# All mixture units of the first two batches run inside the adjacency loop, a slot every second step, and nine groups are combined there

## The reference, cut to what matters

```python
# x: 8192 x 128, adj: 8192 x 8192, all float32
msg = layernorm(x) @ W + B
weights = where(adj < 1.0, exp(-(1/adj - 1)**2 / (2 * 0.5**2)), 0.0)
x = x + weights @ msg
# mixture of experts on layernorm(x): 16 experts, 2 per row, hidden 256
logits = n @ gate_w + gate_b;  top2 = top_k(logits, 2);  share = softmax(top2)
moe = sum_k share_k * (relu(n @ w1[e_k] + b1[e_k]) @ w2[e_k] + b2[e_k])
x = x + layernorm(n + moe) * gamma + beta
```

## Time and profile before

| what | value |
| --- | --- |
| median of 3 runs | 1727.93 us (1727.41 to 1729.02) |
| the profiled execution, its own time | 1725.96 us |
| its span in the trace | 1724.2 us |
| PE busy (matmul) | 1605.5 us, 93% |
| ACT busy | 1563.5 us, 91% |
| DVE busy | 1494.9 us, 87% |
| POOL busy | 538.3 us, 31% |
| mean share of the 16 DMA engines that is busy, q1 | 66.5% |

### The profile page before, as it was taken

One profiled execution on the slowest core, in us unless ns is written; L12 is line 12 of the kernel. 1 busy time (PEld: TensorE's weight loads), 2 busy tenths in 40 slices (PEclk: granted clock), 3 DMA queues, 4 the chain that ended last, 5 costly groups with the idle time before them and its releaser, 6 DMA issues.

```text
span 1724.2 us, 24880 instructions
## 1 busy us (share of the span) xinstructions
PE 1605.5 (93%) x8327; PEld 1069.9 (62%) x8327; DVE 1494.9 (87%) x2312; ACT 1563.5 (91%) x1530; POOL 538.3 (31%) x354
## 2 busy tenths in 40 slices
PE   4999999999999999999999999999998998988870
PEld 3666666666666666656666666666665665757760
DVE  7999989898989898999787878878898898877676
ACT  5899999999999999999999999999997998966662
POOL 1001040404040404090303012040464655465773
PEclk9999999999999999999999999999999999999985
DMA  9558976766666766676777777777776886735662
GB/s 322 150 159 261 259 215 204 207 201 209 201 208 202 208 201 208 200 219 199 216 222 222 216 217 208 220 216 222 226 216 189 239 234 200 228 101 148 183 180 82
DMA packets 246236, 354.26 MB, mean 205 GB/s; under 512 B 20896, under 2 KB 103584, under 8 KB 245984
## 3 DMA queue, kind: packets, MB, share of 16 engines
q1 hardware_dynamic: 237792, 335.62, 66.5%
q0 software_dynamic: 8320, 17.06, 3.2%
HBM read 318.99 MB, written 35.73 MB: 206 GB/s over the span
## 4 chain that ended last, share of the span: by engine, by line
PE 73%; DVE 14%; POOL 4%; issue 4%; ACT 2%; DMA 2%; SPq 1%; DVEq 0%; ACTq 0%; POOLq 0%
PE acc L1394 42%; PE tp L1464 21%; DVE chunk L864 4%; POOL early_back L633 4%; DVE chunk L870 3%; PE tp L1440 2%; PE tp L1431 2%; DVE stats L876 1%; PE tp L1491 1%; DVE chunk L1278 1%; PE acc L1508 1%; ACT chunk L824 1%; PE tp L1508 1%; PE misc L1370 1%; DVE msg L939 1%
## 5 line engine op out<-in xcount | busy, mean ns | idle before, releaser
L1394 PE MATMUL acc<-wT,msg 128*128 128x512 f32 x2048 | 974.3, 598 | 1.8 <-DVE yT L970 1.8
L720 ACT ACTIVATE wT<-tp 128x1024 f32<-128x1024 f32 x512 | 636.4, 1326 | 35.8 <-PE tp L1464 35.7
L870 DVE SCALAR_TENSOR_TENSOR chunk<-chunk 128x2048 f32<-128x2048 f32 x256 | 584.2, 2282 | 31.2 <-ACT chunk L713 30.8
L1464 PEld LDWEIGHTS tp<-ident,chunk 128*128 128x128 f32 x4096 | 478.6, 142 | 204.9 <-issue 199.0
L864 DVE SCALAR_TENSOR_TENSOR chunk<-chunk 128x2048 f32<-128x2048 f32 x256 | 583.7, 2281 | 2.0 <-DMA chunk<-in_adj_dram 2.0
L713 ACT ACTIVATE chunk<-chunk 128x2048 f32<-128x2048 f32 x256 | 567.7, 2217 | 0.1
L1464 PE MATMUL tp<-ident,chunk 128*128 128x128 f32 x4096 | 536.7, 274 | 9.5 <-DVE pair_out L1170 8.7
L1394 PEld LDWEIGHTS acc<-wT,msg 128*128 128x128 f32 x2048 | 351.4, 192 | 255.3 <-issue 249.9
L708 ACT ACTIVATE chunk<-chunk 128x4096 f32<-128x4096 f32 x118 | 466.3, 3951 | 2.3 <-DVE chunk L864 2.3
L673 POOL DMA_INDIRECT rows_in<-y,row_now x128 | 254.4, 1988 | 37.3 <-issue 37.3
L607 POOL TENSOR_TENSOR pool_carrier<-pool_carrier 1x1 f32<-1x1 f32 x32 | 29.8, 931 | 720.7 <-DVE row_now L1055 705.0
(11 more groups left out here) (143 smaller groups left out, 940.7 us busy)
## 6 DMA issues: line engine op xcount, KB each, us to landing
chunk<-in_adj_dram SPq DMA_DIRECT2D x256, 1024.0 KB, 5.7
pair_w<-first_layers SPq DMA_DIRECT2D x104, 129.0 KB, 5.1
pair_in<-rows_in SPq DMA_DIRECT2D x104, 64.0 KB
rows_out<-pair_out SPq DMA_DIRECT2D x52, 128.0 KB, 5.8
chunk<-rows_in SPq DMA_DIRECT2D x85, 64.0 KB
rows_out<-chunk SPq DMA_DIRECT2D x41, 128.0 KB
y_kept<-y SPq DMA_DIRECT2D x16, 256.0 KB, 6.1
rows_in<-zeros SPq DMA_DIRECT2D x64, 64.0 KB
```

The costliest lines, as they stand in the source:

```text
L720: act.activation(wT[:, s % WSLOTS, :], tp[place(s) % TSLOTS][:, :], ACT.Exp, scale=-2.0).then_inc(weighted, 1)
L870: dve.scalar_tensor_tensor(out=slot(c), in0=slot(c), scalar=2.0, in1=slot(c), op0=ALU.subtract, op1=ALU.mult).then_inc(squared, 1)
L1394: ins = pe.matmul(acc[:, :], msg[:, n, :], wT[:, (g * PPG + m) % WSLOTS, k * ROWS:(k + 1) * ROWS], start=(n == 0), stop=(n == 2 * PPG - 1))
L1464: ins = pe.transpose(tp[place(s) % TSLOTS][:, t * ROWS + b * P:t * ROWS + (b + 1) * P], chunk[:, c % RING, b, j:j + P], ident[:, :])
```

## The change

All 128 units of the first two batches (72 and 56, the second padded by one) run in slots, and the slots lie two steps apart: from step 272 to 346 and from 432 to 490. 62 units stay behind the loop. Pair rows are loaded as soon as the buffer of three pairs back is free. Nine groups are combined in the loop, at steps 369 to 509, from three half buffers of four parts each (`ones` and `before`, used at the start only, now lie in one of them); POOL waits for one half at a time. The early guess moves from POOL's power to a logarithm and an exponential on ACT. Behind the loop the positions 0 to 15 hold the last group's gate alone; unit v's output is at position 16 + v, and the seven late groups start at 20, 31, 52, 66, 77, 88 and 99. Rows for the units are loaded from position 7 on.

```diff
-    UNITS[0] += UNITS[0] % 2
+    UNITS = [n + n % 2 if b < 2 else n for b, n in enumerate(UNITS)]
...
-    SLOT_EVERY = 4
-    PAIR_FIRST = [0, UNITS[0] // 2]
-    SECOND_PAIRS = 16
-    NP = PAIR_FIRST[1] + SECOND_PAIRS
+    IN_LOOP = 2
+    SLOT_EVERY = 2
+    PAIR_FIRST = [UNIT0[b] // 2 for b in range(IN_LOOP)]
+    NP = UNIT0[IN_LOOP] // 2
...
-    AT_STEP = [(FIRST[b + 1] + 1) * PPG + 21 for b in range(2)]
+    AT_STEP = [(FIRST[b + 1] + 1) * PPG + 16 for b in range(IN_LOOP)]
+    SLOT_STEP = [AT_STEP[b] + SLOT_EVERY * i for b in range(IN_LOOP) for i in range(UNITS[b] // 2 + 2)]
...
+    ROWS_STEP = [SLOT_STEP[n] - 7 if p < 3 or p - 3 < PAIR_FIRST[pair_batch(p)] else SLOT_STEP[n - 3] + 1
+                 for p, n in enumerate(TURN_SLOT)]
+    WEIGHTS_STEP = [SLOT_STEP[n] - 1 for n in TURN_SLOT]
...
-    EARLY_AT = (436, 461, 471, 493, 503)
-    EARLY_GATE = (12, 13, 13, 14, 14)
+    EARLY_AT = (369, 378, 400, 409, 431, 440, 463, 503, 509)
+    EARLY_GATE = (10, 10, 11, 11, 12, 12, 13, 14, 14)
...
-    EARLY_SLOTS = 8
+    EARLY_HALVES = 3
...
-        early_back = sb("early_back", [P, KB, D])
+        early_back = sb("early_back", [P, EARLY_HALVES, TB, D])
+        ones, before = early_back[:, 0, 0, :], early_back[:, 0, 1, :]
...
+        UNIT_AT = 16
+        ROWS_AT = 7
...
+        starts = dict(zip(LATE, (20, 31, 52, 66, 77, 88, 99)))
...
             def gather_early(h):
-                last_carried()
-                if h == 0:
-                    results_there(0)
-                    pool.wait_ge(idx_ready, 1)
-                else:
-                    pool.wait_ge(early_free, h)
-                carry()
-                gather(h, 0, early_back, early_rows)
...
+                b = max(b for b in range(len(BATCHES)) if FIRST[b] <= h)
+                for k in range(K):
+                    q = K * h + k
+                    last_carried()
+                    if h == FIRST[b] and k == 0:
+                        results_there(b)
+                        pool.wait_ge(idx_ready, b + 1)
+                    if q >= EARLY_HALVES:
+                        pool.wait_ge(early_free, q - EARLY_HALVES + 1)
+                    carry()
+                    for t in range(TB):
+                        gather(h, b, k * TB + t, early_back[:, q % EARLY_HALVES, t, :], early_rows[q % EARLY_HALVES])
...
                     if EARLY_GATE[h] == g:
                         gather_early(h)
-                        guess_early(h)
                 if g == GROUPS - 1:
-                    for late in range(EARLY, FIRST[1]):
-                        gather_late(late)
+                    gather_late(EARLY)
+                    gather_late(EARLY + 1)
...
+            def guess_early(h):
+
+                act.wait_ge(early_moments, h + 1)
+                act.activation(early_lnv[:, :], early_mv[:, :, 1], ACT.Ln, bias=eps[:, 0:1]).then_inc(early_lnv_ready, 1)
+                act.wait_ge(early_lnv_ready, h + 1)
+                act.activation(early_rs[:, :], early_lnv[:, :], ACT.Exp, scale=-0.5).then_inc(early_guessed, 1)
...
+                    for h in range(EARLY):
+                        if g * PPG + m == EARLY_AT[h] + 5:
+                            guess_early(h)
...
-            turn_tile(0)
-            turn_tile(1)
             products(GROUPS - 1, PPG - 2)
-            turn_tile(2)
-            turn_tile(3)
-            hidden(0)
             products(GROUPS - 1, PPG - 1)
-            hidden(1)
-            for i in range(max(NT, PPG)):
+            for i in range(UNIT_AT + NT):
```

More of the change, by code:

```diff
@@ L83, in gnn_moe_kernel @@
     ALL_TURNED = place(STEPS - 1) + 1
-    def pair_batch(p):
-        return 1 if p >= PAIR_FIRST[1] else 0
     NT = NU - NE
@@ L131, in gnn_moe_kernel @@
         ident = sb("ident", [P, P])
-        ones = sb("ones", [P, P])
-        before = sb("before", [P, P])
         eps = sb("eps", [P, 1])
@@ L307, in gnn_moe_kernel @@
         pair_stored = [sem(f"pair_stored{i}") for i in range(2)]
-        early_rows = sem("early_rows")
+        early_rows = [sem(f"early_rows{i}") for i in range(EARLY_HALVES)]
         early_free = sem("early_free")
@@ L551, in _ @@
             for i in range(LAST + 2):
-                if 1 <= i <= NT:
-                    store_rows(i - 1)
-                if i + RIN < NT:
-                    load_rows(i + RIN)
+                if 0 <= i - UNIT_AT - 1 < NT:
+                    store_rows(i - UNIT_AT - 1)
+                if i == ROWS_AT:
+                    for v in range(RIN):
+                        load_rows(v)
+                if RIN <= i - UNIT_AT + RIN < NT:
+                    load_rows(i - UNIT_AT + RIN)
                 if i == 11:
@@ L624, in results_there @@
                 for i in range(2):
-                    pairs = PAIR_FIRST[1] if b == 0 else NP
+                    pairs = (PAIR_FIRST + [NP])[min(b + 1, IN_LOOP)]
                     pool.wait_ge(pair_stored[i], (pairs - i + 1) // 2 * 16)
@@ L664, in gather_late @@
                 carry()
-                gather(g, b, back[h % BACK], back_in[h % BACK])
+                for kb in range(KB):
+                    gather(g, b, kb, back[h % BACK][:, kb, :], back_in[h % BACK])
             def scatter(g):
@@ L681, in _ @@
                         gather_early(h)
-                        guess_early(h)
                 if g == GROUPS - 1:
-                    for late in range(EARLY, FIRST[1]):
-                        gather_late(late)
+                    gather_late(EARLY)
+                    gather_late(EARLY + 1)
                 scatter(g)
-            for g in range(FIRST[1], GROUPS):
+            for g in range(EARLY + 2, GROUPS):
                 gather_late(g)
```

99 lines of the change are left out of this document (40 added, 59 removed).

## The result

The changed kernel takes **1736.06 us** (median of 5 runs, 1735.63 to 1742.19); the kernel before, on the same chip, 1727.93 (1726.12 to 1729.02). The ratio is 1.0056, 95% interval 1.0042 to 1.007: slower by 0.56%. The forecast was 1717.2 with a range of 1702 to 1738, so the range holds the time and the direction was wrong. It came out where the rival "POOL starves under the saturated DVE" had put it, 1736.

What follows compares the result with a forecast made beforehand. PE was taken to bind stretches with slots, ACT those without. Loop -23.1 + 24.0 + 3.6 + 21 + 4 = +29.5 us, last part -40.2, total -10.7 from 1727.93: 1717.2 us, range 1702 to 1738.

Steps and rivals of the forecast that it cites:

- POOL starves under the saturated DVE: Steps 369 to 440: slow gathers and guesses make three combines wait, +19 us, 1736; decides from 30 us per eight gathers; chance 0.17.
- term 5: Loop: new waits for gathered rows, mainly for the combine at step 431, +4 us, between 0 and 7.7.
- term 1: Loop: DVE's stalls for early combines' gathered rows vanish, as gathers begin 10 to 18 steps ahead of use, -23.1 us.
- term 2: Loop: twelve more pairs on PE at 2.00 us each, +24.0 us; 32 steps with sixteen slots take 116.8 us.
- term 3: Loop: 132 steps instead of 216 in slotted stretches, so 84 steps go from 2.65 to 2.69 us, +3.6 us.
- the rival of the dense slots: Slots two steps apart don't run at PE's pace: 30 us more, 1747; chance 0.10.
- term 4: Steps 369 to 426: early combines and the second batch's table overload DVE where no slot hides them, +21 us, bounds 0 and 35.
- The rival that has this overload absorbed: Early combines fit between DVE's chunks, which run ahead, so the overload costs nothing: 1717 - 17 = 1700; chance 0.12.
- ACT's guess "below 0.5 us each: zero": Loop: ACT's two small activations for nine groups lie where DVE or PE binds, below 0.5 us each, so cost zero.
- The last part (129.1): From step 512 to the end: 129.1 us instead of 169.3, so -40.2 us, with POOL's gathers binding at its end.
- the signs named: Profile signs: sixteen slots 116.8 us, steps 352 to 415 about 187, no early_back wait above 5, step 512 near 1584.
- three conditions under which the prediction called itself wrong: Sixteen slots costing over 118 us, POOL's gathers over 30 us a group, or the last part over 140 us.

Runs made afterwards that it cites:

- the fastest kernel: The changed kernel with the first batch's seven combines moved beside dense slots (steps 431 to 485) and group 0's gathers behind group 11's guess: 1708.74 us, ratio 0.9885.
- two of these kernels: Against the changed kernel, early gathers put ahead of guesses: groups 0, 2, 4 (1735.63 us); or groups 0, 3 with seven combines moved beside dense slots (1719.04 us).
- the bench: Not the kernel but a copy of x, with POOL's gathers and small products beside phases of one kind of DVE work; a gather beside nothing took 0.94 us.

## Why the prediction was wrong

The step that failed is term 5: the prediction put the new waits for gathers at 4 us, and they are 22.4 in the trace. The changed kernel's own trace against the terms, between step 256 and the end:

1. *Stalls removed (term 1, -23.1).* The old ones are gone; with the guess back on POOL the waits doubled, so this part of the reasoning held. But it was one sentence too short, see 5.
2. *Pairs on PE (term 2) and fewer slotted steps (term 3).* Right, a little small: 117.73 us for 32 steps where 116.8 was forecast, about 4 us over the 132 slotted steps. No slot waited; the rival of the dense slots is out.
3. *DVE overload (term 4, +21).* Right in size: 18.3 us in steps 352 to 447 by the table above (with what the lower clock costs in them), and some 1.4 more that the fastest kernel still loses there (273.5 against 272.1, which is 80 steps at 86.22 / 32 and 56.6 for steps 432 to 447). The rival that has this overload absorbed takes only 17 us off; to be in line with the term it should take off 21, which gives 1696.
4. *ACT's guess "below 0.5 us each: zero".* No loss on ACT shows in the trace. The worth of taking it off POOL was not: 40 us. I priced the move by the engine it went to and not by the one it left.
5. *New waits for gathers (term 5, +4): **the step that failed.*** They are 22.4 us in steps 352 to 447. I expected one late combine, at 431; the combines of groups 0, 2 and 4, the first of each pair, had to wait. Term 1 gave the gathers "10 to 18 steps" of lead for all groups, and only for the combine at 431 did term 5 look at the moment at which POOL can begin. For group 2 the real order is: POOL idle to 1195.47 behind a guess that DVE releases, 6.6 us of guess and product, then eight gathers and a product until 1229.2, 27 us, for a combine that started at 1222.57.
6. *The threshold of the rival.* It said that starving decides from 30 us for eight gathers. They took 29, 27 and 21 us and it decided: what counts is start plus length, and for group 4 the guess and the product ahead took 13.4 us (1303.31 to 1316.73), the power alone 8.84 of it where it takes 1.06 behind the loop.
7. *The last part (129.1).* 134.9 in the trace. The first output came 21.9 us after step 512 (20 forecast); unit 38 was stored and the gathers began 58.0 after it (54.5), for the wait at 1660.83, which I had taken out as belonging to the kernel before; from there the four groups took 42.1 us, unbroken (42), and the end 12.9 (13):

```profile
1685.52 0.18 POOL L604 TENSOR_TENSOR pool_carrier<-pool_carrier 1x1 f32<-1x1 f32 x1 [23.69 <-DMA rows_out<-chunk]
...
1726.68 0.94 POOL L629 DMA_INDIRECT chunk<-rows_out,row_back  x1 [0.30 <-issue]
```

The sum: 18.4 (term 5) - 1.3 (term 4) + 4 (slots) + 5.8 (last part) = 26.9 us, against 1742.19 - 1715.3 = 26.9 of the profiled execution. Against the median the miss is 18.9; the 6.1 and 2.0 us by which the two traces lie off their medians are in one of these terms or several, and I can't say in which. The kernel with the zero blocks two at a time has the same loop. Its trace shows 22.0 us of these waits and was taken of an execution that also lies 6.1 us above its median. So no trace shows this loop in an execution near the median, and there term 5 may be smaller than 18.4.

Of the signs named, three failed clearly: there are waits above 5 us for `early_back` (8.6, 8.3, 7.1 and 5.5), step 512 is at 1605.6 and not near 1584, and steps 352 to 415 take 196.7 us and not 187. None of the three conditions under which the prediction called itself wrong came true (slots 117.7, a group's gathers 28.7 at most, last part 134.9): they did not look at when POOL begins.

The probabilities: the starving had 0.17. Its mechanism and its price are right (3 x 7.7 us less 4 is 19; measured 18.4). That its 1736 meets the median to a tenth of a microsecond is luck: the other terms were 8.5 us off in the trace, and the two traces' 6.1 and 2.0 us cancel that. The evidence that I weighed against it, that POOL speeds up when DVE waits, is true, and it is the loss itself: by then DVE is waiting. The sentence from the Trainium skill that made term 5 zero was rightly set aside for the row with 3.18 us; but 3.18 was the mild case. Long pieces like the 11.78 and 7.03 of the same rows stood ahead of each of the three waits: 6.81 and 7.02, 6.82 and 7.00, 8.84, 7.80 and 5.26 us.

## What to carry to other kernels

An engine that is 60% busy can still set the pace. Follow the chain that crosses it (DVE's moments, POOL's guess, POOL's gathers, DVE's combine) from its first release to its last use, with each piece at the length it has beside the neighbour that will run then. Before work is moved in an in-order queue, ask what stands behind it; two of these kernels traded a wait for gathers for a wait for a guess. And extra DVE work belongs where PE binds: four combines cost 18.3 us where no slot lay, and brought 14.1 of the 22.4 us of waits there; three cost about 1 us beside dense slots.

## What the runs showed of the hardware

- GpSimd's indirect DMA took 0.94 us alone and 1.81 to 1.90 beside 128x2048 DVE instructions with two SBUF inputs. Single ones were held until DVE's run was over: 13.6, 19.7, 22.5 and 24.7 us beside two SBUF inputs, 22.2 beside a `tensor_scalar` with one. In the kernels single ones took 5.3 to 11.8.
- A 1x1 product on GpSimd took 0.18 us alone, 7.00 in the loop and 26.87 in the bench; a 128x4 power 1.05 alone and 8.84 in the loop.
- Beside DVE instructions with an input in PSUM, reductions and statistics, gathers stayed at 0.94 to 1.05 us.
- Copies and `tensor_scalar` of 128x2048 with one SBUF input both ran at 1.14 us each on DVE; the one delayed each gather to 1.97 us, the other held one for the rest of its run. Why they differ was not found.
- After 10.6 us in which PE only waited, the granted clock of the stretch was 0.81 and one step's matmuls took 1.92 and 3.23 us instead of 1.04 and 1.88.
